# Another order of the work of VectorE, GpSimd and the DMA queue in a hybrid attention kernel

## What is computed

```python
x = x + _L0_attn_a_ref(_layernorm(x))   # linear attention: softmax(q) . (softmax(k)^T v), 16 heads of 64
x = x + _L0_ffn_ref(_layernorm(x))      # r * (relu(k)^2 @ W_v), r = sigmoid(...), inputs mixed with the token before
x = x + _L0_attn_b_ref(_layernorm(x))   # softmax attention with rope, 16 heads of 8
x = x + _L0_ffn_ref(_layernorm(x))
```

## Time and profile before

| | before |
|---|---|
| median of 3 runs | 1030.16 us (1025.34 to 1038.49) |
| the profiled execution | 1037.24 us, its span 1035.4 us |
| busy: PE, DVE, ACT, POOL | 910.1 (88%), 726.8 (70%), 674.0 (65%), 594.6 (57%) us |
| mean granted TensorE clock | 0.963 of 2.4 GHz |
| DMA | 87.63 MB, mean 85 GB/s, 28.0% of 16 engines' span |

### The profile page before, as it was taken

One profiled execution on the slowest core, in us unless ns is written; L12 is line 12 of the kernel. 1 busy time (PEld: TensorE's weight loads), 2 busy tenths in 40 slices (PEclk: granted clock), 3 DMA queues, 4 the chain that ended last, 5 costly groups with the idle time before them and its releaser, 6 DMA issues.

```text
span 1035.4 us, 24352 instructions
## 1 busy us (share of the span) xinstructions
PE 910.1 (88%) x9743; PEld 535.8 (52%) x9743; DVE 726.8 (70%) x1494; ACT 674.0 (65%) x657; POOL 594.6 (57%) x425
## 2 busy tenths in 40 slices
PE   5986979999998989989898999989999999878983
PEld 3775535555564556555454655545555555433332
DVE  5777626867886787878778687877868678554144
ACT  4555746767765767666666767666677667657870
POOL 3748455747766584757657475765758556442200
PEclk9999989999999999999999999999999999989996
DMA  5013142324132233323223332312332331413210
GB/s 163 19 32 113 42 130 67 101 62 128 60 110 84 82 104 89 106 60 119 59 82 108 88 103 60 120 57 83 111 95 83 92 104 51 124 44 120 70 44 14
DMA packets 68684, 87.63 MB, mean 85 GB/s; under 512 B 13649, under 2 KB 40146, under 8 KB 68562
## 3 DMA queue, kind: packets, MB, share of 16 engines
q1 hardware_dynamic: 68562, 85.96, 28.0%
HBM read 16.19 MB, written 20.97 MB: 36 GB/s over the span
## 4 chain that ended last, share of the span: by engine, by line
PE 47%; DVE 18%; POOL 8%; SPq 7%; ACT 6%; issue 6%; DMA 5%; POOLq 0%; DVEq 0%; ACTq 0%
PE PS L1723 14%; PE PS L1679 7%; DVE cT L1189 4%; PE PS L1518 4%; DMA parted<-U 4%; SPq L343 3%; PE PS L1586 3%; PE PS L1513 3%; PE PS L1520 3%; PE PS L1519 3%; ACT work L748 2%; DVE mom L956 2%; SPq L333 2%; POOL rs L482 2%; PE PS L1632 2%
## 5 line engine op out<-in xcount | busy, mean ns | idle before, releaser
L748 ACT ACTIVATE work<-PS 128x2048 f32<-128x2048 f32 x150 | 282.0, 1880 | 161.4 <-PE PS L1679 161.4
L748 ACT ACTIVATE work_b<-PS 128x2048 f32<-128x2048 f32 x74 | 139.1, 1880 | 72.3 <-PE PS L1679 72.3
L1723 PE MATMUL PS<-work,v 128*32 128x512 f32 x1368 | 182.8, 628 | 0.5 <-ACT work L755 0.5
L738 ACT ACTIVATE work<-PS 128x512 f32<-128x512 f32 x256 | 148.7, 597 | 50.9 <-PE PS L1520 48.5
L482 POOL TENSOR_TENSOR rs<-ve,half_neg 128x4 f32<-128x4 f32 x64 | 64.8, 1012 | 176.2 <-DVE ve L960 175.3
L1518 PE MATMUL PS<-wqk,h1h 128*128 128x512 f32 x256 | 127.0, 496 | 28.6 <-DVE qkv_sb L1088 18.3
L495 POOL TENSOR_TENSOR work<-work,q_rcp 128x1024 f32<-128x1024 f32 x64 | 125.9, 1967 | 32.5 <-DVE q_rcp L1014 32.5
L1679 PE MATMUL PS<-q_st,k_st 32*128 32x512 f32 x896 | 117.2, 512 | 12.9 <-DMA q_st<-qk_lo 5.0
L1520 PE MATMUL PS<-wqk,h1l 128*128 128x512 f32 x256 | 103.3, 404 | 0.0
L1519 PE MATMUL PS<-wqk,h1h 128*128 128x512 f32 x256 | 103.1, 403 | 0.0
L508 POOL TENSOR_TENSOR mask_cos<-qkv_sb,cos_t 128x1024 f32<-128x1024 f32 x16 | 38.0, 2374 | 104.7 <-DVE qkv_sb L1088 103.4
(11 more groups left out here) (181 smaller groups left out, 1757.4 us busy)
## 6 DMA issues: line engine op xcount, KB each, us to landing
qkv_scratch<-qkv_sb SPq DMA_DIRECT2D x16, 768.0 KB, 5.1
rot<-qkv_sb SPq DMA_DIRECT2D x32, 256.0 KB, 3.1
k_st<-qk_hi SPq DMA_DIRECT2D x128, 64.0 KB, 2.1
q_st<-qk_hi SPq DMA_DIRECT2D x128, 64.0 KB, 2.1
k_st<-qk_lo SPq DMA_DIRECT2D x128, 64.0 KB, 2.1
q_st<-qk_lo SPq DMA_DIRECT2D x128, 64.0 KB, 2.1
parted<-U SPq DMA_DIRECT2D x52, 128.0 KB, 3.0
xa<-in_attn_a_x SPq DMA_DIRECT2D x16, 256.0 KB, 3.1
```

Source lines behind the costliest of these rows:

```text
L738: act.activation((EQ, EK)[r // 2][c % 2][:, (r % 2) * 512:(r % 2) * 512 + 512], PS[:, bank, :], ACT.Exp)\
L748: act.activation(probs_of(z, b, n), PS[:, 0:4, :], ACT.Exp).then_inc(z["s_exp"].sem, 1)
L1723: mm = pe.matmul(PS[32 * h:32 * h + 32, 6, :], v_flat[p][:, kc, at:at + 32], probs_of(z, b, n)[:, h, :], start=(n % 8 == 0), stop=(n % 8 = ...
```

## The change

Nothing is computed otherwise, and no instruction is added or taken away; SP's and POOL's and DVE's instructions stand in another order, and two waits come with the moved DMAs. In a full iteration:

- DVE: `sums_of(a, 0)` and `ln1_stats(a + 1)` move from behind `m_copy` to behind the second `p_copy`; the third `p_copy` (v) goes ahead of `divide`; the two `look_at` reductions go behind `m_copy`; `sums_of(a, 1)` goes behind `c_add(a, 0)` and `h1_copy`; `x3_stats` goes ahead of k's `relu`.
- POOL: `q_hats(a, 0)` goes between the product with the cosines and that with the sines; `v_copy` goes from behind the square to behind `ln_apply` of xa; `split_lo` (L528) goes from ahead of the square to behind `q_hats(a, 2)`.
- SP: the eight DMAs of the next batch's group 0 go ahead of x2's store, the four from `qk_hi` first, each four behind its own half of the split.

```diff
-            def first_stacks(z):
+            def first_stacks(z, j):
 
+                hold(sp, z["s_mm"], j, -4)
                 for part, rows in ((qk_hi, ((1, 0), (1, 2), (0, 0), (0, 1))), (qk_lo, ((1, 1), (1, 3), (0, 2), (0, 3)))):
-                    hold(sp, z["split"], 0, 1 if part is qk_hi else 2)
+                    hold(sp, z["split"], j, 1 if part is qk_hi else 2)
...
@@ SP, paired_step
+                first_stacks(z, l)
                 store_x2(s)
-                stack_k(z, l, 0)
-                stack_q(z, l, 0)
@@ POOL, paired_step
                     rope_by_cos(z, l)
+                    if A:
+                        q_hats(a, 0)
                     rope_by_sin(z, l)
                     rope_sum(z, l)
-                if A and E:
-                    q_hats(a, 0)
                 if there(a + 1):
                     rsqrt_var(0, a + 1)
                     ln_apply(0, a + 1, xa, h1, h1_T)
+                if E:
+                    hold(pool, p_ev, l)
+                    hold(pool, z["pv"], l - 2)
+                    v_copy(z, l, p)
...
-                split_qk(z, l)
+                split_hi(z, l)
                 hold(pool, f1["v"], s - 1)
                 square(f1, s)
-                if not E and there(a + 1):
-                    split_h1(a + 1, 1 - p)
-                hold(pool, p_ev, l)
-                hold(pool, z["pv"], l - 2)
-                v_copy(z, l, p)
                 if E:
                     rsqrt_var(3, e)
                     ln3_apply(e)
                 if A:
                     q_hats(a, 2)
+                split_lo(z, l)
+                if not E:
+                    hold(pool, p_ev, l)
+                    hold(pool, z["pv"], l - 2)
+                    v_copy(z, l, p)
+                if not E and there(a + 1):
+                    split_h1(a + 1, 1 - p)
                 rsqrt_var(2, s)
@@ DVE, paired_step
                     p_copy(l, 1, other)
+                    if A:
+                        sums_of(a, 0)
+                    if there(a + 1):
+                        ln1_stats(a + 1)
+                    p_copy(l, 2, 5 if A else 4)
                     divide(z, e)
-                    p_copy(l, 2, 5 if A else 4)
-                    look_at(parted[:, 1, :], e, AX_X, 2)
...
                 m_copy(s, 7)
-                if A:
+                if E:
+                    look_at(parted[:, 1, :], e, AX_X, 2)
+                if A and not E:
                     sums_of(a, 0)
-                if there(a + 1):
+                if not E:
                     ln1_stats(a + 1)
                 add_x1(s, 7 if A else 5)
...
                 if A:
-                    sums_of(a, 1)
                     c_add(a, 0)
                 if E and there(a + 1):
                     h1_copy(a + 1, 1 - p)
+                if A:
+                    sums_of(a, 1)
...
                 pv_copy(z, b, 0)
+                if E:
+                    x3_stats(z, 3, e)
                 hold(dve, f2["act"], e - 1)
                 relu(f1, s, other)
-                if E:
-                    x3_stats(z, 3, e)
```

More of the change, by code:

```diff
@@ L378, in filling_step @@
                     store_qkv(l)
-                    first_stacks(att[0])
+                    first_stacks(att[0], l)
                 if there(s):
@@ L519, in split_qk, with split_hi @@
             def split_qk(z, j):
+                split_hi(z, j)
+                split_lo(z, j)
+            def split_hi(z, j):
                 for g in range(2):
@@ L526, in split_qk, with split_lo @@
                                    ALU.mult).then_inc(z["split"].sem, 1)
+            def split_lo(z, j):
                 hold(pool, z["split"], j, 1)
```

## The result

The changed kernel takes 982.11 us (median of 4 runs, 980.77 to 983.2) against 1034.3 us for the kernel before (4 runs, 1025.34 to 1038.49): a ratio of 0.9506, with a 95% interval of 0.9432 to 0.958. The range of the prediction (978 to 1018) holds it and its side was right, but the gain was 52 us where 35 were forecast.

What follows compares the result with a forecast made beforehand. TensorE's program plus its waits bounds the kernel; 62.9 us of waits on DVE and POOL, less 27.8 not gained, gives 35.1 us: 1002 profiled, 995 by the median. Range 978 to 1018, favoured band 985 to 1005 (chance 0.56).

Steps and rivals of the forecast that it cites:

- The mechanism: DVE and POOL reordered so TensorE stops waiting: v's copy comes 1.88 us earlier in late iterations; back-half waits go.
- the rival of one catch more: Statistics ahead of v's copy caught by the sines in all twelve full iterations: 20 us gained, 1010 us; chance 0.20.
- M: M's copy, now behind the division, delays attn_out by 0.5 us in each of iterations 8 to 15: 4.0 us lost.
- The high half: Back half, POOL: at worst it catches x3's statistics; the square then ends at 439.0, 0.6 us ahead of TensorE.
- The low half: Moved later on POOL, it ends about 446.5; its DMAs land about 451.5, 4 us of cover left: cost 0.
- The 967 us for all 62.9 gained: Whole kernel without any catch or new wait: all 62.9 us of TensorE's listed waits go.
- q's second scaling: At the contexts, it ends 0.6 to 0.7 us too late behind h1's copy: 0.7 in twelve iterations, 8.4 us lost.
- Iterations 4 to 7: Swapped pairs land early: v's waits stay (3.0), M's copy 1.1 later four times, 7.4 us; plus 5.0 for further catching.
- third catch: Iterations 4 to 7: POOL's sum also catches the last small statistics operation, 2.5 us each; half of 10 us counted.
- Iterations 3 and 16: Their chains have other lengths, so some 3 us of the waits were left in them as not gained.
- The Trainium skill's lock rule: Shared VectorE and GpSimd port blocks the second comer for a whole instruction; gain 35 us by it, 45 (985) otherwise.

Runs made afterwards that it cites:

- seventh experiment: Changed kernel with POOL's low half of the split put back right behind the high half, ahead of the square: 1017.64 us, ratio 0.9814.
- ninth kernel: Changed kernel with q's first scaling between sines and sum, M's copy inside the division, and the two looks at parted ahead of v's copy: 960.08 us.
- eleventh experiment: Changed kernel with q's second sums on DVE put back ahead of the addition of contexts and h1's copy: 982.06 us, ratio 0.945.
- first experiment: Changed kernel with q's first scaling on POOL put back behind rope's sum: 968.43 us, ratio 0.930.
- second experiments: Changed kernel with q's first scaling on POOL between the product with the sines and the sum: 965.1 us, ratio 0.9288.
- sixth experiment: Changed kernel with the statistics of x3 put back behind k's relu: 973.6 us, ratio 0.940.
- the tenth: Kernel with scaling between sines and sum, M's copy inside the division, looks ahead of v's copy, plus x3's statistics behind k's relu: 964.89 us, ratio 0.9296.

## Why the prediction was right, and where its sum was not

**The mechanism** held. The waits for the square, the third addition and the norm of x3 left, all but 2.0 us, and the late iterations ran as drawn, to within some tenths. The last small operation, L972, ends at 404.45, 0.04 us ahead of the sines, where the prediction had 0.2; it started 0.20 us ahead, and that a start was enough was the argument that kept the rival of one catch more from coming true. M was late by 0.29 us in iteration 8 and by 6.7 us in nine waits, 2.1 of them in iteration 16, so 4.6 in eight (4.0). In the back half, iteration 8:

```profile
424.89 1.90 POOL L529 TENSOR_TENSOR qk_hi<-mask_cos,one 128x1024 fp32r<-128x1024 f32 x1 [0.62 <-DMA q_st<-qk_lo]
424.95 1.86 DVE L968 TENSOR_SCALAR mom<-mom 128x4 f32<-128x4 f32 x1
...
427.07 0.69 DVE L1104 TENSOR_SCALAR k_relu<-PS 128x512 f32<-128x512 f32 x1
...
427.90 1.04 POOL L505 TENSOR_TENSOR k_act<-k_relu 128x512 f32<-128x512 f32 x1 [1.12 <-DVE k_relu L1104]
...
429.94 1.16 PE L1657 MATMUL PS<-W7T,k_act 128*128 128x128 f32 x8
```

The high half catches the statistics once, as at worst foreseen, and the square ends at 428.94, 1.0 us ahead of TensorE (0.6 forecast). The low half starts at 434.42, its four DMAs are issued from 436.84 to 439.22, and the next scores start at 445.8 without a wait: cost 0, as said. The seventh experiment shows that this move carries the change.

**The term that was not there: TensorE's busy time, 14.0 us.** The sum took 62.9 us of waits as the most that could be had and let the matmuls keep their durations. But the busy time of TensorE fell as well, by 13.5 us in iterations 8 to 15. Over the whole span, TensorE was busy for 61.0 us at the lower level before and for 42.6 us after; half of the difference, 9.2 us, is an estimate of what the clock gave of the 14.0, and the other 4.8 us stay open. The page before already had five of eight iterations below 1.00, with busy times of 54.9 to 56.4 us beside 53.0 to 53.4 in the three at 1.00; I never compared them. The 967 us for all 62.9 gained was therefore no bound: the ninth kernel, another order of the same work, took 960.08. Its profile has 25.1 us of busy time less than that of before and 51.7 us of idle time, so it went below with fewer than 62.9 us of waits.

**q's second scaling: 8.4 us forecast, 1.8 measured.** The size was wrong because I measured slack at the wrong row. The earlier trace rows give the weight load (PEld) at 431.92, and I took that for TensorE's arrival. The timeline of before has the matmul 0.43 us later:

```profile
432.35 0.63 PE L1586 MATMUL PS<-work 128*32 128x64 f32 x32
```

Against the 432.5 at which I had the scaling end, that would have been 0.15 us. In the changed kernel's iteration 8:

```profile
422.02 0.52 PEld L1604 LDWEIGHTS PS<-work 128*32 128x32 f32 x32 [1.05 <-issue]
422.05 0.65 PE L1604 MATMUL PS<-work 128*32 128x64 f32 x32 [0.17 <-POOL work L495]
```

The load unit was idle for 1.05 us, but the matmuls that stand ahead of it were running until 0.17 us before its start; only the 0.17 is lost. Eleven such waits make 1.8 us, and the eleventh experiment, which removes them, gained nothing that shows.

**Iterations 4 to 7: right place, wrong make-up.** I priced them at 7.4 + 5.0 us not gained: v's waits of 3.0 left, 4 x 1.1 at M, and half a chance of a third catch at 2.5 each. The third catch came in all four; TensorE waits 3.1 us each time for v's copy (12.5), and so not at all for M's. In waits, 12.4 forecast and 12.5 measured agree, but by chance: all catches at full price would have been 17.4. What came on top is the clock again, two more stretches of 3.4 us at the lower level (four, where two were before). Their busy time rose by 1.8 us, with the same work (us, busy PE, PEld, DVE, ACT, POOL, clock); before:

```profile
166.40:401.10 234.70, 216.39 (x2508) 129.65 (x2508) 182.06 (x364) 162.32 (x146) 153.18 (x109) 0.99 0.30 90
```

and after:

```profile
159.80:392.20 232.40, 218.23 (x2509) 130.32 (x2508) 190.38 (x364) 161.93 (x146) 153.53 (x109) 0.97 0.30 90
```

The prediction saw that filling POOL's gap takes away the moment at which DVE gets through, and did not draw the consequence; the first experiment did: leave the gap open, and 14 us come.

**Iterations 3 and 16** gave 7.7 and 5.0 us. The 3.0 us left in them as lost were too cautious for iteration 3, whose whole 3.9 us at the contexts went; in iteration 16 2.1 us stayed, 1.8 for the norm of x3 and 0.3 more than before for M. **Filling and draining** cost 2.5 us more, which I had not priced; the traces place it at both ends (1.1 and 1.3 us) and I have not traced it to an instruction.

The sum, on the profiled executions: 27.8 us of waits were to stay and 21.2 stayed (4.6 for 4.0 at M, 12.5 for 12.4 in iterations 4 to 7, 1.8 for 8.4 at q's scaling, 2.3 for 3.0 for the rest). So 41.7 us of waits went where 35.1 were forecast, and the 6.6 between are q's scaling. 0.4 us of idle time came in elsewhere, and the 14.0 us of busy time had no term. So the step that carried the forecast off its size is that q's term was too large and this one missing; both lay on the same side.

**The Trainium skill's lock rule** (SBUF — State Buffer, in "SBUF: two separate sides") was used at one place: whoever comes second at the shared port is blocked for the other's whole instruction. The trace agrees: 1.87, 2.28 and 2.23 us for three operations in iteration 5, 0.15 to 0.17 for the same ones in the first experiment.

## What to carry to other kernels

Where one engine's short operations are caught by another's long ones, the idle gaps of the long one are what the short ones live on: place the series so that it falls into such a gap, and do not fill the gap with work that can go elsewhere. Before summing up waits, compare TensorE's busy time and granted clock over equal pieces of work; where they differ, removing the waits can also buy clock, and the sum of the waits is not the bound. Measure the slack of a matmul at the matmul's row, not at its weight load's.

## What the runs showed of the hardware that was not expected

**A long wait goes with half clock.** Each of the four waits of 3.1 us in the changed kernel is followed by a stretch of 3.4 us at the lower level, 1.2 GHz (clock 0.50 in the last but two column). The stretch behind that of iteration 5, TensorE having been idle from 231.9 to 235.04:

```profile
235.30:238.70 3.40, 3.40 (x15) 1.07 (x18) 3.37 (x2) 1.35 (x1) 3.23 (x4) 0.50 0.00 0
```

The others start at 177.3, 293.3 and 351.4, and from 392 to 824 there is none. In all traces together there are 21 waits of 3.1 us for v's copy, and 20 go with a stretch of 3.4 or 6.8 us at the lower level, which begins within the wait or at most 1.7 us behind its end. The exception is iteration 5 of the eleventh experiment: TensorE is idle from 233.30 to 236.44, and the clock stays at 1.00. The first and second experiments have no such wait and no such stretch in these iterations. In the kernel before, three stretches follow waits of 1.9 to 2.1 us for v's copy (536.3, 597.8, 717.2), five more in its full iterations (212.1, 328.1, 505.6, 567.0, 686.5) start 0.6 to 5.3 us behind a wait of 1.3 to 2.0 us for the square or the norm of x3, and other waits of 1.8 to 2.2 us are followed by none. So a wait of 3.1 us nearly always cost its clock, one of 2 us sometimes. This is read from where they stand; no run changed the clock alone.

**What is caught.** In these traces TENSOR_TENSOR and TENSOR_SCALAR on 128x4 tiles in SBUF and the division's 128x512 product are caught (0.16 us becomes up to 2.35; the division's product, which always has POOL beside it, takes 0.97 to 2.61 in the changed kernel, 1.48 in iteration 8), the copies out of PSUM (0.69), the reciprocal (3.34), the sums (1.21) and the BN statistics (0.81 for four) are not, beside the same instructions of POOL. The form of the operation alone does not tell: a TENSOR_TENSOR that reads one operand from PSUM (L1038, 0.41 to 0.43 in all 52 of 128x256) is not caught, and a SCALAR_TENSOR_TENSOR on 128x512 with both in SBUF (L1120, 0.69 alone) takes up to 2.25. A series of seven small operations can be caught once for each instruction of POOL that starts in it, not once in all.

**A small packet goes with a late landing.** The swapped pairs (2 x 256 KB) decide whether there is a gap. In the DMA view of the sixth experiment, around its iteration 5 (packets, MB, share of 16 engines; KB each, median us to landing):

```profile
q8 instruction: 1, 0.02, 2.3%
...
rot<-qkv_sb SPq DMA_DIRECT2D x2, 256.0 KB, 3.5
```

In the changed kernel's iteration 5, the packet begins only at 228.43, 10.4 us into the iteration; in the window 225.4 to 228.3 it is not yet there, and the issues' row is

```profile
rot<-qkv_sb SPq DMA_DIRECT2D x2, 256.0 KB, 2.9
```

Its iteration 8, with late pairs, has the packet 8.8 us into the iteration (3.6 us). Most of the difference is in the second transfer of the pair: it lands 3.0 us behind the start of its issue in iteration 5, 4.1 us in iteration 8 and 4.3 us in the sixth experiment's iteration 5.

Of the 156 full iterations of all 13 traces, 106 have this packet, of 16 KB, at 9.9 us or earlier, and in all of them the pairs landed late (11.5 to 13.3 us into the iteration); 33 have it at 10.3 us or later, and in all of them they landed early (10.5 to 11.2). In the 17 between, 13 landed early (10.4 to 11.1), and the four late ones (12.8 to 13.3) are iterations 5 and 7 of the sixth experiment and 6 and 7 of the tenth. So just where the sixth experiment differs from the changed kernel, the packet's place in the iteration does not tell early from late; there the pair was also issued 0.4 to 0.5 us later than in the changed kernel (8.0 us for 7.5). What the landing decides is shown, a catch and 3 us of TensorE. That the packet delays it is a correlation over iterations: no run moved the packet by itself, and why the sixth experiment shifted the landing stays open.
